# Convolution in 64x64 tiles: block states of odd channels computed across the array's halves

## The chip, the cores and the metric

The kernel runs on one core of one Trainium2 chip. The metric is the device time of one execution in microseconds (us). Three executions of the kernel before took 973.1, 973.68 and 978.77 us; their median is 973.68 us.

## The reference, cut to what matters

The input `x` is [8, 512, 256] (batch, steps, channels). A recurrence of 512 steps makes `u`. Then each channel of `u` goes through a causal convolution whose kernel is a sum of 64 decaying exponentials, and the result and a skip term are added to `x`:

```python
_, hs = jax.lax.scan(step, h0, jnp.swapaxes(xw, 0, 1))       # u: 512 steps, tanh
...
at = dt[:, None, None] * A[None, None, :] * t[None, :, None]
K = jnp.einsum('mn,mln->ml', C_re, jnp.exp(at))              # kernel of each channel
u_f = jnp.fft.rfft(u.transpose(0, 2, 1), n=2 * L_)
k_f = jnp.fft.rfft(K, n=2 * L_)
y = jnp.fft.irfft(u_f * k_f, n=2 * L_)[..., :L_]
return y.transpose(0, 2, 1) + u * D
...
x = x + _L0_attn_ref(_L0_cond_ref(x, ...), ...)
x = x + _L0_ffn_ref(_L0_cond2_ref(x, ...), ...)              # gated recurrence, then experts
```

The convolution is the part that the change touches.

## The kernel before, in words

The kernel is written with one instruction list per engine and semaphores between them, so the order in each list is the order in which that engine works. The stages are: the recurrence (products of 128x32 tiles, about 7 to 378 us), the convolution (about 379 to 448 us), the gated recurrence with routing and the shared network, and the 16 experts.

For the convolution the 512 steps of a batch are cut into 8 blocks of 64 steps (`HB`). The 256 channels are two halves of 128 (`k`), held in partitions 0 to 63 and 64 to 127 of one tile: partition rows are the 64 steps of a block, `rows_of_half(k)`. Channels are taken 8 at a time (`CP`), in 16 groups (`NCH`); the group's parity `z` picks the buffers. TensorE works with the array split into four tiles of 64x64; a tile is named by (its rows' start, its columns' start). The rows decide from which partitions it reads, the columns to which partitions of PSUM it writes. A float32 product of the program appears as two products in the trace. For each group of channels TensorE does three blocks of work:

- `own_block(z)` (L590): the block's own steps against a 64x64 Toeplitz matrix, 8 channels x 2 halves x even and odd blocks, 32 columns each. All four tiles are used in turn.
- `block_states(1 - z)` (L577): for the next group, the 64 state terms that each block leaves behind, 8 channels x 2 halves, 56 columns each. Half 0 uses tile (0, 0) and half 1 tile (64, 64); the other two tiles are not used. It writes bank 0 or bank 1 of PSUM, by the parity.
- `carried(z)` (L599): the states that come from earlier blocks, added onto the sums of `own_block`, 32 columns each, in all four tiles.

Between `block_states` and `carried` of a group VectorE carries the states over the blocks by a scan (`carry`, L1169), and after `carried` it adds the sums to `x` (`add_x`, L1175). One `block_states` stands ahead of the loop. GpSimd and ScalarE make the powers and decays of later groups (L393, L404, L892) and copy operands into the two slots that the loop can address (L897, L902); SyncE moves the Toeplitz matrices into their slots (L336). Each of the three blocks is led by `stand()` (L604): a product of zeros, 128 rows, 32 columns of the array, 8 columns streamed, that carries the semaphore wait.

Ahead of the loop 64 transposes of 128x128 (L565) turn the recurrence's output, and VectorE (L1160) and ScalarE (L905) copy it out of PSUM by turns. At the start of the kernel one DMA loads `pack`, a row of small operands, on ScalarE's queue.

Of the kernel before, what the change touches and what calls it, by code (L numbers as in the profile page):

```python
# [13 lines left out]
P = 128  # L14
B, S, D = 8, 512, 256
C = D // P
# [37 lines left out]
def build(nc, x_tok, x_steps, h0_gate, wx_d, wh_d, b_rec_d, pack_d,  # L54
# [5 lines left out]
    with ExitStack() as ctx:  # L60
# [3 lines left out]
        def sem(name):  # L64
            return ctx.enter_context(nc.semaphore(name))
# [5 lines left out]
        sizes = (C * B, NST, 1, P + KP, P, IT, KP * C * KP, 8, HB, RB, R + CT)  # L71
        pack = sb("pack", [P, sum(sizes)])
        h0r, a_bc, a_q, dt_q, c_q, d_k, masks, consts, iota_t, resets_t, rows_to = [pack[:, sum(sizes[:n]):sum(sizes[:n + 1])] for n in range(len(sizes))]
# [158 lines left out]
        s_own = sem("s_own")  # L232
        s_slot_tz = [sem("s_slot_tz0"), sem("s_slot_tz1")]
# [6 lines left out]
        block = ctx.enter_context(nc.Block())  # L240

# [142 lines left out]
        def _(pool):  # L384
# [7 lines left out]
            def power_args(m):  # L392
                pool.tensor_tensor(pw[:, m % 2], dt_q[:, CP * m:CP * m + CP].unsqueeze(2).to_broadcast([P, CP, NST]),  # L393
                                   a_bc.unsqueeze(1).to_broadcast([P, CP, NST]), ALU.mult).then_inc(s_pa, 1)
# [5 lines left out]
            pool.wait_ge(s_dtm, 3)  # L400
            for m in range(2):
                power_args(m)
            def block_decays(m):
                pool.tensor_tensor(d0[:, m % 2], lam[:, CP * m:CP * m + CP].unsqueeze(2).to_broadcast([P, CP, RB]),  # L404
                                   resets_t.unsqueeze(1).to_broadcast([P, CP, RB]), ALU.mult).then_inc(s_d0, 1)
# [72 lines left out]
        def _(pe):  # L478
# [115 lines left out]
            def carried(z):  # L594

                for c in range(CP):
                    for k in range(C):
                        for odd in range(2):
                            last = nc.tensor.matmul(to_tokens(z, c, k, odd), qd[rows_of_half(k), CP * z + c], xc[rows_of_half(k), z, c].rearrange("p (r e) -> p r e", e=2)[:, :, odd],  # L599
                                                    start=False, stop=True, skip_group_check=True, tile_position=(HB * k, HB * odd))  # L600
                last.then_inc(s_qmm, 1)
# [260 lines left out]
        def _(act):  # L862
# [6 lines left out]
            nc.scalar.activation(dt_q[:], dt_q[:], ACT.Exp).then_inc(s_dtm, 1)  # L869
            act.wait_ge(s_dta, 1)  # L870
# [245 lines left out]
        def _(dve):  # L1116
# [42 lines left out]
            nc.vector.memset(ps[:, 0:2].rearrange("p n (c t) -> p (n c) t", t=NB)[:, :, 0], 0.0).then_inc(s_xc, 1)  # L1159
# [332 lines left out]
```

## Time and profile before

| What | Value |
|---|---|
| median of three runs | 973.68 us (973.1 to 978.77) |
| the profiled execution's own time | 974.19 us |
| span in the profile, mean granted clock | 972.3 us, 0.978 |
| TensorE products busy | 924.3 us (95%) |
| VectorE, ScalarE, GpSimd busy | 410.7 (42%), 506.3 (52%), 299.1 us (31%) |
| recurrence, about | 7 to 378 us |
| transposes and copies | 379 to 388 us |
| convolution loop | 388 to 448 us |

The span is the time from the first to the last instruction; 1.9 us of the profiled execution lie around it. Busy times are sums over an engine's instructions; weight loads are counted apart as PEld and lie beside the products. "PEclk" in the profile is the clock that TensorE was granted, in parts of full speed: 1.00 is 2.4 GHz, 0.50 is 1.2 GHz.

### The profile page before, as it was taken

Reading aid. Unit: us, or ns where it says so; the run is one execution under the profiler, and the core shown is the slowest. Engines: PE = TensorE matmul, PEld = TensorE weight load, DVE = VectorE, ACT = ScalarE, POOL = GpSimd, SP = SyncE. Lnnn points to the kernel's source line nnn. Section 1 sums busy time; section 2 is a strip of 40 time slices with the busy share of each in tenths; the row PEclk is TensorE's granted clock in tenths of the full one; section 3 lists DMA queues with packets and bytes.
Section 4 is the critical chain, followed back from the end, with each engine's and each line's share of the span. In section 5 each row is a group of like instructions: output and inputs, shape, how many; then the busy total and the mean of one; then the engine's idle time right before and its main releaser. Section 6 shows DMA issues by size and latency. Waiting matters only on the chain.

```text
span 972.3 us, 64880 instructions
## 1 busy us (share of the span) xinstructions
PE 924.3 (95%) x28864; PEld 777.5 (80%) x28864; DVE 410.7 (42%) x781; ACT 506.3 (52%) x1735; POOL 299.1 (31%) x324
## 2 busy tenths in 40 slices
PE   7999999999999999999999998999899999999993
PEld 5888888888888888996444446788899999999993
DVE  1000010100001103553899799875564646556450
ACT  2444444444444446443876587134465656566551
POOL 3111111111111110650003463760045364554545
PEclk6799999999999999999999999999999999999997
DMA  2222222221111111111001110533357666675634
GB/s 89 83 92 87 95 93 87 100 85 33 35 40 36 35 33 28 66 76 57 0 1 39 49 56 22 184 116 108 127 132 162 133 157 119 151 146 127 134 40 53
DMA packets 69161, 80.34 MB, mean 83 GB/s; under 512 B 24225, under 2 KB 53558, under 8 KB 69122
## 3 DMA queue, kind: packets, MB, share of 16 engines
q1 hardware_dynamic: 54242, 62.18, 20.3%
q0 software_dynamic: 14592, 17.10, 10.7%
q8 instruction: 23, 0.38, 0.2%
q10 hardware_dynamic: 288, 0.56, 0.2%
q14 instruction: 16, 0.13, 0.0%
HBM read 44.16 MB, written 33.83 MB: 80 GB/s over the span
## 4 chain that ended last, share of the span: by engine, by line
PE 81%; issue 5%; ACT 4%; POOL 4%; DVE 3%; DMA 2%; POOLq 0%; SPq 0%; ACTq 0%; DVEq 0%
PE ps L516 19%; PE ps L811 16%; PE ps L508 9%; PE ps L825 8%; PE ps L677 8%; PE ps L489 6%; PE ps L727 3%; POOL slots_in L447 2%; PE ps L577 2%; ACT tok L879 2%; PE ps L590 2%; PE ps L736 2%; PE ps L599 2%; PE ps L494 2%; DMA slots_in<-tok,arena 1%
## 5 line engine op out<-in xcount | busy, mean ns | idle before, releaser
L516 PE MATMUL ps<-tok,wh 128*32 128x8 f32 x16384 | 255.2, 180 | 12.9 <-issue 3.5
L879 ACT ACTIVATE tok<-ps 128x8 f32<-128x8 f32 x1024 | 155.9, 177 | 204.0 <-PE ps L516 201.6
L516 PEld LDWEIGHTS ps<-tok,wh 128*32 128x32 f32 x16384 | 220.0, 113 | 48.0 <-ACT tok L879 25.2
L466 POOL DMA_INDIRECT out<-arena,dest x80 | 127.9, 1599 | 99.3 <-ACT arena L1030 76.9
L489 PE MATMUL ps<-zero 128*32 128x192 bf16 x1920 | 141.1, 255 | 0.0
L418 POOL TENSOR_TENSOR big<-tok,zero 128x128 f32 x64 | 29.0, 453 | 322.0 <-ACT tok L879 322.0
L811 PE MATMUL ps<-xgT_hi,ew_hi 128*128 128x320 f32 (+1 forms) x384 | 119.5, 311 | 3.2 <-DVE spare L1275 1.6
L811 PE MATMUL ps<-xgT_hi,ew_lo 128*128 128x320 f32 (+1 forms) x384 | 119.5, 311 | 0.0
L811 PE MATMUL ps<-xgT_lo,ew_hi 128*128 128x320 f32 (+1 forms) x384 | 119.0, 310 | 0.0
L1143 DVE TENSOR_TENSOR arena<-arena,pack 128x256 f32 x32 | 13.6, 426 | 246.3 <-ACT arena L884 246.3
L1381 DVE TENSOR_TENSOR mid<-mid,ps 128x320 f32<-128x320 f32 (+1 forms) x96 | 46.6, 486 | 107.0 <-ACT mid L1048 57.5
L677 PE MATMUL ps<-mid,gw 128*128 128x512 f32 x192 | 83.8, 593 | 2.5 <-ACT mid L958 1.6
L447 POOL DMA_INDIRECT slots_in<-tok,arena x64 | 73.1, 1142 | 23.6 <-issue 17.1
L1048 ACT ACTIVATE mid<-ps 128x320 f32<-128x320 f32 (+1 forms) x96 | 41.8, 435 | 73.9 <-PE ps L811 71.0
L508 PE MATMUL ps<-xst,wx 128*32 128x64 f32 (+1 forms) x3120 | 76.3, 209 | 0.0
L677 PEld LDWEIGHTS ps<-mid,gw 128*128 128x128 f32 x192 | 36.1, 190 | 46.5 <-issue 45.2
L811 PEld LDWEIGHTS ps<-xgT_hi,ew_hi 128*128 128x128 f32 (+1 forms) x384 | 69.2, 180 | 4.0 <-DVE spare L1275 1.9
L825 PE MATMUL ps<-ew_hi,eact_hi 128*128 128x256 f32 (+1 forms) x240 | 71.7, 299 | 0.3 <-ACT arena L1030 0.3
L489 PEld LDWEIGHTS ps<-zero 128*32 128x32 bf16 x1920 | 62.1, 96 | 11.5 <-issue 0.5
L811 PEld LDWEIGHTS ps<-xgT_lo,ew_hi 128*128 128x128 f32 (+1 forms) x384 | 69.4, 181 | 0.0
L811 PEld LDWEIGHTS ps<-xgT_hi,ew_lo 128*128 128x128 f32 (+1 forms) x384 | 69.3, 180 | 0.0
L825 PE MATMUL ps<-ew_lo,eact_hi 128*128 128x256 f32 (+1 forms) x240 | 67.8, 282 | 0.0
(206 smaller groups left out, 1643.5 us busy)
## 6 DMA issues: line engine op xcount, KB each, us to landing
slots_in<-mid SPq DMA_DIRECT2D x16, 645.0 KB, 3.7
mid<-slots_in SPq DMA_DIRECT2D x16, 645.0 KB, 4.2
arena<-in_ex_down SPq DMA_DIRECT2D x16, 384.0 KB
arena<-in_ex_gate SPq DMA_DIRECT2D x16, 352.0 KB
arena<-in_ex_up SPq DMA_DIRECT2D x16, 352.0 KB
xst<-in_x_steps SPq DMA_DIRECT2D x66, 64.0 KB, 1.8
xtok<-in_x_tok SPq DMA_DIRECT2D x16, 256.0 KB, 2.7
mid<-k_pad SPq DMA_DIRECT2D x32, 128.0 KB, 3.1
```

The source lines that it names most:

```text
L447: pool.indirect_dma_start(out=slots_in[:, :], out_offset=bass.IndirectOffsetOnAxis(ap=idx[:, k, r:r + 1], axis=0), in_=hid_tok[:, r, :], i ...
L466: pool.indirect_dma_start(out=out[:, :], out_offset=bass.IndirectOffsetOnAxis(ap=dest[:, z, t:t + 1], axis=0), in_=yo[:, z, t], in_offset= ...
L489: nc.tensor.matmul(ps[Q * j:Q * j + Q, 6, 0:columns], zero16[:, 0:Q], zero16[:, 0:columns], start=True, stop=True, tile_position=(0, Q * j))
L508: last = nc.tensor.matmul(ps[Q * j:Q * j + Q, to, 0:cols], w, v, start=c < 0, stop=c == C - 1, skip_group_check=True, tile_position=(0, Q ...
L516: last = nc.tensor.matmul(sums_at(bank, t, o)[Q * j:Q * j + Q], wh[:, k, columns(j, o)], hring[:, (n - 1) % (2 * G), k], start=False, stop ...
L677: last = nc.tensor.matmul(ps[:, gate_bank(n % NT, q), :], gw[:, q, c, z * P:(z + 1) * P], x1T[:, c, 4 * b:4 * b + 4, :].rearrange("p r t - ...
L727: last = nc.tensor.matmul(ps[0:fw, bank, :], of(w)[:, c, f0:f0 + fw], v, start=c == 0 and p == 0, stop=c == C - 1 and p == len(parts) - 1)
L811: last = nc.tensor.matmul(ps[0:fw, 2 * h + m % 2, 0:HALF], of(w)[:, c, f0:f0 + fw], v[:, c, hf * HALF:(hf + 1) * HALF], start=c == 0 and p ...
L825: last = nc.tensor.matmul(ps[:, 4 + (z + t) % 2, 0:D], a[0:fw, f, t * P:(t + 1) * P], down_of(w)[0:fw, f], start=f == 0 and p == 0, stop=f ...
L879: nc.scalar.activation(hring[:, n, o], sums_at(n // G, n % G, o), ACT.Tanh).then_inc(s_h[o], 1)
L1048: nc.scalar.activation(esil[0:fw, m % 2], ps[0:fw, m % 2, 0:HALF], ACT.Silu).then_inc(s_esil, 1)
L1381: nc.vector.tensor_tensor(eprod[0:fw, m % 2], esil[0:fw, m % 2], ps[0:fw, 2 + m % 2, 0:HALF], ALU.mult).then_inc(s_eact, 1)
```

## The change

The states of odd channels of a group are now computed in the two tiles that stood still: half 0 writes to partitions 64 to 127 and half 1 to partitions 0 to 63. So that two row halves never add into one bank at a time, the even channels' states lie in one bank and the odd ones' in the next (banks 0 and 1 for even groups, 6 and 7 for odd ones), and `carried` is split into the even and the crossed channels. Between the two parts the states of the next group are computed. Decays, kernels and masks of odd channels are laid out with their halves exchanged, for which `pack` gets 128 more columns (`dt_s`, the step sizes not exchanged) and ScalarE one more exponential. The wait product is now 128x128 with 128 columns and adds zeros to columns of a sum's bank that hold nothing. Ten products of zeros with 256 columns follow the transposes, and VectorE clears two more banks once the first transposes are done.

```diff
+        psf = ps[:, :, :].rearrange("p n t -> p (n t)")
+        def states_at(z):
+            return psf[:, 512 * 6 * z + 256:512 * 6 * z + 768]
+        def place_of(c):
+            return CP // 2 * (c % 2) + c // 2
...
-            pool.wait_ge(s_dtm, 3)
+            pool.wait_ge(s_dtm, 4)
...
+            pe.wait_ge(s_xc, 1)
+            for _ in range(5):
+                nc.tensor.matmul(ps[:, 0, 0:256], zero16[:, 0:P], zero16[:, 0:256], start=True, stop=True)
+                nc.tensor.matmul(ps[:, 0, 0:256], zero16[:, 0:P], zero16[:, 0:256], start=True, stop=True)
...
                 for c in range(CP):
                     for k in range(C):
-                        to = ps[rows_of_half(k), z, RB * c:RB * c + RB].rearrange("p (b t) -> p b t", t=NB)[:, :, 1:NB]
+                        h, at = k ^ c % 2, RB * place_of(c)
+                        to = states_at(z)[rows_of_half(h), at:at + RB].rearrange("p (b t) -> p b t", t=NB)[:, :, 1:NB]
                         last = nc.tensor.matmul(to, pw[rows_of_half(k), z, c], u_tok[rows_of_half(k), CP * z + c].rearrange("p (b t) -> p b t", t=NB)[:, :, 0:NB - 1],
-                                                start=True, stop=True, skip_group_check=True, tile_position=(HB * k, HB * k))
+                                                start=True, stop=True, skip_group_check=True, tile_position=(HB * k, HB * h))
...
-            def carried(z):
-                for c in range(CP):
-                    for k in range(C):
+            def carried(z, crossed):
+                for c in range(crossed, CP, 2):
+                    for h in range(C):
                         for odd in range(2):
...
+                last.then_inc((s_half, s_qmm)[crossed], 1)
...
-            def stand():
-                nc.tensor.matmul(ps[0:Q, 6, 0:B], zero16[:, 0:Q], zero16[:, 0:B], start=True, stop=True, tile_position=(0, 0))
+            def stand(z):
+                at = R * CP
+                nc.tensor.matmul(ps[:, 2 + 2 * z, at:at + P], zero16[:, 0:P], zero16[:, 0:P], start=False, stop=False, skip_group_check=True)
...
-                    stand()
+                    stand(z)
                     own_block(z)
+                    pe.wait_ge(s_xc, m + 2)
                     pe.wait_ge(s_pe, m + 2)
-                    pe.wait_ge(s_xc, m + 1)
                     pe.wait_ge(s_uea, 2 * m + SLOTS - 1)
-                    stand()
+                    stand(z)
+                    carried(z, 0)
                     block_states(1 - z)
-                    pe.wait_ge(s_xc, m + 2)
-                    pe.wait_ge(s_uea, 2 * m + SLOTS - 2)
-                    stand()
-                    carried(z)
+                    pe.wait_ge(s_half, m + 1)
+                    stand(z)
+                    carried(z, 1)
...
+            nc.scalar.activation(dt_s[:], dt_s[:], ACT.Exp).then_inc(s_dtm, 1)
...
-            nc.vector.memset(ps[:, 0:2].rearrange("p n (c t) -> p (n c) t", t=NB)[:, :, 0], 0.0).then_inc(s_xc, 1)
+            nc.vector.memset(ps[:, 0:2].rearrange("p n (c t) -> p (n c) t", t=NB)[:, :, 0], 0.0)
+            dve.wait_ge(s_utr, 1)
+            nc.vector.memset(ps[:, 6:8].rearrange("p n (c t) -> p (n c) t", t=NB)[:, :, 0], 0.0).then_inc(s_xc, 1)
...
-                nc.vector.tensor_tensor_scan(xc[:, z].rearrange("p c r -> p (c r)"), d0[:, z].rearrange("p c r -> p (c r)"), ps[:, z, :], 0.0, ALU.mult, ALU.add).then_inc(s_xc, 1)
+                nc.vector.tensor_tensor_scan(xc[:, z].rearrange("p c r -> p (c r)"), d0[:, z].rearrange("p c r -> p (c r)"), states_at(z), 0.0, ALU.mult, ALU.add).then_inc(s_xc, 1)
```

This is TensorE's list for one group of channels (`z` = 0) in the loop before. L604 is `stand`, L590 `own_block`, L577 `block_states`, L599 `carried`:

```order
L604 MATMUL ps<-zero 32x8 [waits s_slot_tz0]
L590 MATMUL ps<-tok,mid 64x32 x32
L619 REGISTER_ALU
L621 ISA [waits s_xc,s_pe]
L604 MATMUL ps<-zero 32x8 [waits s_uea]
L577 MATMUL ps<-tok,arena 64x8x7 x16
L625 REGISTER_ALU [waits s_xc]
L604 MATMUL ps<-zero 32x8 [waits s_uea]
L599 MATMUL ps<-arena 64x32 x32
```

And the same group in the changed kernel, where L621 is `stand`, L605 `own_block`, L614 `carried` and L592 `block_states`:

```order
L621 MATMUL ps<-zero 128x128 [waits s_slot_tz0]
L605 MATMUL ps<-tok,mid 64x32 x32
L636 REGISTER_ALU
L638 ISA [waits s_pe,s_xc]
L621 MATMUL ps<-zero 128x128 [waits s_uea]
L614 MATMUL ps<-arena 64x32 x16
L592 MATMUL ps<-tok,arena 64x8x7 x16
L621 MATMUL ps<-zero 128x128 [waits s_half]
L614 MATMUL ps<-arena 64x32 x16
```

The counts of products in the blocks are the same. Half of `carried` now stands ahead of the states without a wait product between them, and the wait for the scan of this group has moved from behind the states to ahead of them.

On VectorE, at the passage from the recurrence to the convolution, the list of the changed kernel reads as follows; the second row is new, and all eight copies stand behind it:

```order
L1177 MEMSET ps 128x128 [waits s_h1,s_h0]
L1179 MEMSET ps 128x128 [waits s_utr]
L1180 COPY tok<-ps 128x128x4 [waits s_utr] x8
L1189 SCALAR_TENSOR_TENSOR arena<-arena,ps 128x512 [waits s_d0,s_tmm,s_x]
L1189 SCALAR_TENSOR_TENSOR arena<-arena,ps 128x512 [waits s_d0,s_tmm]
L1195 TENSOR_TENSOR xtok<-ps,xtok 128x2x32x8 [waits s_qmm]
```

## Rows read from the trace of the kernel before

**Rows 1.** Windows by stage: stretch, length, busy us (records) of each engine, PEclk, DMA, GB/s.
```profile
7.70:35.00 27.30, 22.51 (x1049) 20.28 (x1050) 1.32 (x5) 8.08 (x51) 3.62 (x6) 0.50 0.17 55
35.00:62.00 27.00, 26.29 (x1729) 22.52 (x1731) 2.68 (x11) 12.37 (x81) 3.99 (x8) 1.00 0.30 105
...
379.00:388.00 9.00, 7.64 (x64) 7.43 (x64) 7.47 (x8) 7.74 (x10) 0.32 (x1) 1.00 0.01 2
388.00:448.00 60.00, 58.37 (x2640) 54.60 (x2640) 29.66 (x32) 27.66 (x45) 29.41 (x28) 1.00 0.17 62
```

**Rows 2.** Timeline of a period of the loop: start, length, engine, line, operation, count.
```profile
400.58 0.18 PE L604 MATMUL ps<-zero 128*32 128x8 bf16 x1
...
400.69 1.14 PE L590 MATMUL ps<-tok,mid 64*64 64x32 f32 x64
...
400.72 0.69 DVE L1175 TENSOR_TENSOR xtok<-ps,xtok 128x512 f32<-128x512 f32 x1
...
401.75 0.18 PE L604 MATMUL ps<-zero 128*32 128x8 bf16 x1
...
401.86 1.14 PE L577 MATMUL ps<-tok,arena 64*64 64x56 f32 x32
...
402.93 0.18 PE L604 MATMUL ps<-zero 128*32 128x8 bf16 x1
...
403.04 1.14 PE L599 MATMUL ps<-arena 64*64 64x32 f32 x64
403.05 1.22 DVE L1169 TENSOR_TENSOR_SCAN arena<-arena,ps 128x512 f32<-128x512 f32 x1 [1.64 <-PE ps L577]
```

**Rows 3.** Waits from 384 to 452 us: who waits for whom, us, times, longest.
```profile
PE ps L577 <- DVE tok L1160: 1.2, 1, 1.2
```

**Rows 4.** Groups of TensorE products, 374 to 452 us: busy, mean ns, idle before.
```profile
L577 PE MATMUL ps<-tok,arena 64*64 64x56 f32 x544 | 19.4, 221 | 1.2 <-DVE tok L1160 1.2
```

**Rows 5.** TensorE alone in equal stretches inside one `own_block`, then one `block_states`.
```profile
389.50:390.08 0.58, 0.58 (x49) 1.00 0.00 0
390.70:391.28 0.58, 0.58 (x25) 1.00 0.00 0
```

**Rows 6.** Timeline of products in tiles of 128x32: the router's, then the recurrence's.
```profile
501.30 1.07 PE L662 MATMUL ps<-big,rw 128*32 128x256 f32 x16 [0.26 <-ACT mid L920]
```
```profile
374.40 0.27 PE L489 MATMUL ps<-zero 128*32 128x192 bf16 x4
...
374.49 0.43 PE L516 MATMUL ps<-tok,wh 128*32 128x8 f32 x32
```

**Rows 7.** Weight loads of full width and of the wait product: ns min/median/max.
```profile
L484 PEld LDWEIGHTS ps<-zero x8: 105/147/147, 1.3 to 3.9; 128*128 128x128 bf16 x8
```
```profile
L604 PEld LDWEIGHTS ps<-zero x48: 92/92/93, 389.2 to 446.5; 128*32 128x32 bf16 x48
```

**Rows 8.** DMA issues, 388 to 452 us: KB each, median us to landing.
```profile
mid<-mid SPq DMA_DIRECT2D x14, 256.0 KB, 2.3
```

**Rows 9.** Timeline ahead of the loop.
```profile
378.79 0.17 DVE L1159 MEMSET ps<- 128x128 f32 x1 [5.13 <-ACT tok L879]
...
379.38 7.64 PE L565 MATMUL ps<-ident,big 128*128 128x128 f32 x64 [0.91 <-POOL big L418]
380.13 7.47 DVE L1160 COPY tok<-ps 128x512 f32<-128x512 f32 x8 [1.17 <-PE ps L565]
380.57 7.50 ACT L905 ACTIVATE tok<-ps 128x512 f32<-128x512 f32 x8 [1.26 <-PE ps L565]
...
388.18 1.14 PE L577 MATMUL ps<-tok,arena 64*64 64x56 f32 x32 [1.16 <-DVE tok L1160]
```

**Rows 10.** Start of the kernel: issues of the first 6 us, then the timeline.
```profile
pack<-in_pack ACTq DMA_DIRECT2D x1, 289.0 KB, 3.0
```
```profile
4.03 0.30 ACT L869 ACTIVATE pack<-pack 128x132 f32<-128x132 f32 x1
...
5.50 0.18 PEld L508 LDWEIGHTS ps<-spare,brow 1*32 1x32 f32 x8 [1.50 <-issue]
```

More of the change, by code:

```diff
@@ L70, in build @@
         h0g = sb("h0g", [P, C, B])
-        sizes = (C * B, NST, 1, P + KP, P, IT, KP * C * KP, 8, HB, RB, R + CT)
+        sizes = (C * B, NST, 1, P + KP, P, P, IT, KP * C * KP, 8, HB, RB, R + CT)
         pack = sb("pack", [P, sum(sizes)])
-        h0r, a_bc, a_q, dt_q, c_q, d_k, masks, consts, iota_t, resets_t, rows_to = [pack[:, sum(sizes[:n]):sum(sizes[:n + 1])] for n in range(len(sizes))]
+        h0r, a_bc, a_q, dt_q, dt_s, c_q, d_k, masks, consts, iota_t, resets_t, rows_to = [pack[:, sum(sizes[:n]):sum(sizes[:n + 1])] for n in range(len(sizes))]
         h0r = h0r.rearrange("p (c b) -> p c b", c=C)
@@ L232, in build @@
         s_own = sem("s_own")
+        s_half = sem("s_half")
         s_slot_tz = [sem("s_slot_tz0"), sem("s_slot_tz1")]
@@ L392, in power_args @@
             def power_args(m):
-                pool.tensor_tensor(pw[:, m % 2], dt_q[:, CP * m:CP * m + CP].unsqueeze(2).to_broadcast([P, CP, NST]),
+                pool.tensor_tensor(pw[:, m % 2], dt_s[:, CP * m:CP * m + CP].unsqueeze(2).to_broadcast([P, CP, NST]),
                                    a_bc.unsqueeze(1).to_broadcast([P, CP, NST]), ALU.mult).then_inc(s_pa, 1)
@@ L403, in block_decays @@
             def block_decays(m):
-                pool.tensor_tensor(d0[:, m % 2], lam[:, CP * m:CP * m + CP].unsqueeze(2).to_broadcast([P, CP, RB]),
-                                   resets_t.unsqueeze(1).to_broadcast([P, CP, RB]), ALU.mult).then_inc(s_d0, 1)
+                pool.tensor_tensor(d0[:, m % 2].rearrange("p (e c) r -> p e c r", e=2), lam[:, CP * m:CP * m + CP].rearrange("p (c e) -> p e c", e=2).unsqueeze(3).to_broadcast([P, 2, CP // 2, RB]),
+                                   resets_t.unsqueeze(1).unsqueeze(1).to_broadcast([P, 2, CP // 2, RB]), ALU.mult).then_inc(s_d0, 1)
             pool.wait_ge(s_lam, 1)
@@ L592, in own_block @@
                 last.then_inc(s_own, 1)
-            def carried(z):
-                for c in range(CP):
-                    for k in range(C):
+            def carried(z, crossed):
+                for c in range(crossed, CP, 2):
+                    for h in range(C):
                         for odd in range(2):
-                            last = nc.tensor.matmul(to_tokens(z, c, k, odd), qd[rows_of_half(k), CP * z + c], xc[rows_of_half(k), z, c].rearrange("p (r e) -> p r e", e=2)[:, :, odd],
-                                                    start=False, stop=True, skip_group_check=True, tile_position=(HB * k, HB * odd))
-                last.then_inc(s_qmm, 1)
-            def stand():
-                nc.tensor.matmul(ps[0:Q, 6, 0:B], zero16[:, 0:Q], zero16[:, 0:B], start=True, stop=True, tile_position=(0, 0))
+                            last = nc.tensor.matmul(to_tokens(z, c, h ^ crossed, odd), qd[rows_of_half(h), CP * z + c], xc[rows_of_half(h), z, place_of(c)].rearrange("p (r e) -> p r e", e=2)[:, :, odd],
+                                                    start=False, stop=True, skip_group_check=True, tile_position=(HB * h, HB * odd))
+                last.then_inc((s_half, s_qmm)[crossed], 1)
+            def stand(z):
+                at = R * CP
+                nc.tensor.matmul(ps[:, 2 + 2 * z, at:at + P], zero16[:, 0:P], zero16[:, 0:P], start=False, stop=False, skip_group_check=True)
             pe.wait_ge(s_uev, NB)
@@ L1446, with crossed @@
     masks = np.zeros((P, KP, C, KP), f32)
-    masks[:, np.arange(KP), :, np.arange(KP)] = (half[:, None] == np.arange(C))[None]
+    masks[:, np.arange(KP), :, np.arange(KP)] = (half ^ np.arange(KP)[:, None] % 2)[:, :, None] == np.arange(C)
     over = np.zeros((P, KP), f32)
+    def crossed(v):
+        w = v.reshape(C, P, -1).copy()
+        w[:, 1::2] = w[::-1, 1::2]
+        return w
     steps = x.reshape(B, S // G, G // 2, 2, C, P).transpose(1, 5, 4, 3, 2, 0).reshape(S // G, P, C, G, B)
@@ L1457 @@
     tri = np.stack([np.triu(np.ones((P, P)), 1) - 1, np.ones((P, P))], 1).astype(f32)
-    pack = (rows(cond.T), np.broadcast_to(a_log, (P, NST)), np.tile(a_log, C), np.concatenate([np.repeat(dt.reshape(C, P), HB, 0), over], 1),
-            c_re.reshape(C, P, NST).transpose(0, 2, 1), d_k, masks, consts, np.broadcast_to(-np.arange(HB, dtype=f32), (P, HB)),
+    pack = (rows(cond.T), np.broadcast_to(a_log, (P, NST)), np.tile(a_log, C), np.concatenate([np.repeat(crossed(dt)[:, :, 0], HB, 0), over], 1), np.repeat(dt.reshape(C, P), HB, 0),
+            crossed(c_re).transpose(0, 2, 1), d_k, masks, consts, np.broadcast_to(-np.arange(HB, dtype=f32), (P, HB)),
             np.broadcast_to((np.arange(RB) % NB > 0).astype(f32), (P, RB)),
```

## The prediction

> **What bounds the kernel now.** I read the windows by stage first. In the loop of the convolution, 388 to 448 us, TensorE is busy 58.37 of 60.00 us and every other engine under 30 [rows 1], and its granted clock is 1.00, the level of 2.4 GHz. So the stage lasts as long as TensorE's list. The view of waits agrees: the one wait of this stage's products is 1.2 us ahead of the first states [rows 3].
>
> The timeline of one period tells what the list costs [rows 2]. A wait product starts at 400.58, the own block at 400.69, the next wait product at 401.75, the states at 401.86, the next at 402.93, the carried block at 403.04. Each block with its wait product takes 1.17 to 1.18 us, of which 0.11 lie between the wait product's start and the block's. Three make a period of 3.53 us.
>
> The point is that 64 products of `own_block` and 32 of `block_states` both last 1.14 us. Less the 0.22 us of the last one (its mean is 221 ns [rows 4]), 0.92 us lie between the first start and the last: 0.92/63 = 14.6 ns for each product of the own block, 0.92/31 = 29.7 ns for each of the states. In equal stretches, 49 records stand against 25 [rows 5]. A turn over the tiles, four in one case and two in the other, takes 58 or 59 ns either way. The states' turn is as long although its products have 56 columns and not 32, so the columns are not what sets it, and two tiles stand still.
>
> **The change part by part.**
>
> *States in four tiles.* If a turn stays at 58 ns and holds four products, 32 products take 32 x 14.6 = 0.47 instead of 32 x 29.7 = 0.95 us: 0.48 less. 544 products [rows 4] are 17 blocks of 32, so 8.2 us less. The least saving is zero (the tiles run as pairs, below). More would need a turn under 58 ns, which neither block shows. Can four tiles stream 56 columns at once? The nearest rows say yes: 16 router products of 256 float32 columns in four tiles last 1.07 us together, the last one included [rows 6]. At 4 turns that is under 0.27 us a turn for 256 columns, so 56 columns in four tiles fit into 58 ns. And the own block reads both row halves for both column halves. I take 0.47 a block, 8.0 us, for the turn that starts a block is a little longer.
>
> *Wait products of 128 columns.* There are 48 before [rows 7] and 48 after, three to a group: the count of passages between the full array and the 64x64 tiles stays. Each streams 120 columns more. Four products of 192 columns hold the array for 0.09 us (374.40 to 374.49 [rows 6]), 0.47 ns a column with the passage, so 120 columns are 0.05 us, and 48 x 0.05 = 2.5 us more. Lower bound: nothing, if the columns run under the 0.11 us that each passage takes. Upper bound: 96 more weight columns at the same rate, 0.04 each, so 0.09 and 4.3 us. I take 2.5, since the weight load of full width takes 105 ns at least where that of 32 columns takes 92 [rows 7], 13 ns apart and not 40.
>
> The Trainium skill (TensorE: Matmul & The Clock Gate, LDWEIGHTS) puts a load at its columns divided by 1.2 ns: 107 for 128 and 27 for 32, 80 ns apart. By that the sum would lose 3.8 us more, and the gain would nearly go; the 13 ns between the two rows speak against it, in durations that hold the whole load.
>
> *The order of the list.* The products of a group are the same; half of `carried` and the states run on without a wait product between them. What moves is the wait for the scan. Before, the states' products of group m ended, and the scan (1.22 us, started about 0.26 after the last states' product: 401.86 + 0.92 = 402.78 against 403.05 [rows 2]) had a carried and an own block and more to run under. After the states of group m TensorE now has: passage 0.15, wait product 0.16, half a carried block 0.45, passage and wait product 0.31, own block 0.92, passage 0.15. That is 2.1 us (0.15 is 401.75 less 400.69 less 0.92; 0.16 is 0.11 plus 0.05). The scan is done after 0.26 + 1.22 + about 0.1 = 1.6 us. So 0.5 us remain, and the wait costs nothing in the steady loop. For the first group, where no carried block comes between, 0.15 + 0.16 + 0.92 + 0.15 = 1.4 us stand against 1.6: 0.2 us once. `add_x` (0.69 us) follows each scan, ends 2.3 us after the states and is not needed for 4 us; both together are 1.9 of a period of 3.2, so VectorE doesn't bound. The slot copies of the Toeplitz matrices land 2.3 us after their issue [rows 8] and have two periods less one block, 5.3 us. The wait for the even half is for products that ended 0.6 us earlier.
>
> *Zeros behind the transposes.* TensorE has 64 transposes at 379.38 for 7.64 us, so they end at 387.02, and the states start at 388.18 when ScalarE's copy, which ends at 388.07, is done [rows 9]. Ten products of 256 columns at 0.47 ns are 1.2 us. They can start a little before the last transpose ends, as the wait product at 401.75 does before the own block's end at 401.83 [rows 2], so at 386.9, and end at 388.1, with 0.1 for the passage to the tiles at 388.2: they fit, or are 0.1 late. Cover: ScalarE's last copy. I charge nothing, at most 0.2. The clearing of two more banks is 0.17 us ahead of VectorE's eight copies [rows 9]. VectorE's last copy then ends at 387.8, before ScalarE's 388.07; the transposes of later turns wait for it and can push ScalarE by at most 0.2. I take 0.1.
>
> *Start.* `pack` grows by 128 columns, 64 KB beside 289 [rows 10]. At that load's own rate (289 KB in 3.0 us) it is 0.66 us, an upper bound for the loads that TensorE's first product at 5.50 waits for; the exponential (0.30 us for 132 columns) stands on ScalarE 1.5 us before the first tanh can come. I take 0.2 us, bounds 0 and 0.7.
>
> **Sum**: -8.0 + 2.5 + 0.2 + 0.1 + 0.2 = -5.0 us. Against the profiled execution's 974.19 that is 969.2; the median of the runs shown is 0.5 lower, so **969.0 us**. Its own range, by the bounds of the wait products and the start: 966 to 972.
>
> **Rivals.**
>
> 1. *The tiles run as pairs* (slower). The four products of a turn write two banks, two row halves into each. If tiles of both row halves can't work into a bank at the same time, or the crossed tiles wait for the straight ones, a turn of four costs two turns of 58 ns and the states stay at 0.95. Then only the costs remain: +3.0 us, 976.7. The point from which the change loses is 3.0/17 = 0.18 us saved in a block. Against it: before, the two tiles of the states already write one bank from both row halves at the same turn as the own block. The Trainium skill (TensorEngine Tiling (Array Packing), Gotcha 1) says that "different row tiles cannot access same PSUM bank simultaneously"; by it the changed states would still go one half at a time, 976.7. The 25 records of [rows 5] don't look like it, but can't exclude it. Chance 13%.
> 2. *The wait products are dear*: at the upper bound of 0.09 us each, -8.0 + 4.3 + 0.5 = -3.2, so 970.5; with the dearer load of the page's rule about 972.8. Chance 12%.
> 3. *The clock*. At 0.50, the level of 1.2 GHz, 27.3 us held 1049 products where 27.0 us at 1.00 held 1729 [rows 1]: a stretch at half costs up to 0.4 to 0.5 of its length. Should the denser loop lose the clock for some microseconds, that is 1 to 3 us, so 970 to 972; should the slow stretch at the start, 27.3 us long and worth 10.7 us, end sooner or later in these runs, 966 or 972. Nothing in the stage hints at it: 1.00 before, in the transposes and in the loop. Chance 9%.
> 4. *A wait of the order*: if the scan or its release were 0.6 us later than I reckon, each period would be bound by it, and 16 periods lose 0.1 to 0.3 us each, 971 to 974. Chance 6%.
>
> **How the numbers follow.** The forecast has 60%. With its own 966 to 972, rivals 2 and 3 and most of 4, the range 965.5 to 975.5 leaves out rival 1 and the tails. Measured differences under 1% (9.7 us) can't be told from no change here; the run shown at 978.77 is 5 us off its neighbours. Faster by over 1% (under 964) needs the forecast and a shorter slow stretch at the start: 5%. Slower by over 1% (over 983.4) needs rival 1 and a lost clock: 3%. Within 1%: 92%.
>
> **What the profile of the changed kernel would show.** Right: the states' line with 32 products in about 0.7 us instead of 1.14, a period of 3.2 us instead of 3.53, wait products 0.16 ahead of their blocks, no TensorE wait for the scan but the first, the first states at 388.2 to 388.5, PEclk 1.00. Wrong: states still near 1.1 us (rival 1), wait products 0.2 ahead of their blocks (rival 2), "idle before" on the wait product with the scan as releaser (rival 4), or digits below 9 in PEclk between 379 and 445 us (rival 3).

## The result and the profile after

The changed kernel takes 1008.34 us (median of four executions, 1005.3 to 1010.01), the kernel before 973.9. The ratio is 1.033, 95% interval 1.029 to 1.037. The prediction of 969.0 with a range of 965.5 to 975.5 was wrong, and wrong in sign. One more thing is needed to read the numbers below: executions of one kernel can differ by 25 us and more, by whether TensorE's clock is lost in the loop.

The page of the changed kernel's profile shows where to look: a hole in TensorE's granted clock in the middle of the kernel, under a row of nines for its busy time (40 slices of 25.2 us, tenths).

```profile
PE   7999999999999999999999999999899999999994
...
PEclk6599999999999999555899999999999999999997
```

In windows that end where the clock changes (the others where the stage or the row of before does; stretch, length, busy us and records of PE, PEld, DVE, ACT, POOL, then PEclk, DMA share, GB/s):

```profile
7.70:35.00 27.30, 21.57 (x1007) 19.26 (x1006) 1.33 (x5) 7.75 (x48) 3.63 (x6) 0.50 0.17 55
35.00:52.00 17.00, 17.00 (x826) 15.38 (x818) 1.16 (x6) 5.92 (x39) 2.19 (x5) 0.50 0.21 72
```
```profile
393.37:400.20 6.83, 5.92 (x283) 5.16 (x285) 3.02 (x3) 3.25 (x6) 4.21 (x4) 1.00 0.12 41
400.20:480.50 80.30, 79.27 (x2371) 70.55 (x2363) 27.16 (x29) 24.63 (x39) 25.22 (x24) 0.50 0.12 43
480.50:488.95 8.45, 7.35 (x15) 3.86 (x16) 0.29 (x1) 1.20 (x2) 0.00 (x0) 0.50 0.39 132
```

The loop of the convolution starts at full clock, loses it at 400.2 us after seven microseconds and never gets it back: to the end of the loop and 8 us into the next stage TensorE stands at 0.50, the level of 1.2 GHz, busy for 79.27 of 80.30 us. The loop before had 1.00 throughout [rows 1]. In this execution the stretch at half clock at the start was also longer, 44.4 us where it was 27.3 [rows 1]; most of the 5.1 us by which the transposes start later (384.45 against 379.38 [rows 9]) goes with that. The loop's part is larger: from its first states to the next stage's first transposes it takes 87.5 us (393.37 to 480.85), and the time before was 60.4 (388.18 [rows 9] to 448.59). The next stage's first transposes, in the changed kernel, then before:

```profile
480.85 1.97 PE L653 MATMUL ps<-ident,xtok 128*128 128x128 f32 x8 [0.81 <-DVE xtok L1195]
```
```profile
448.59 1.09 PE L636 MATMUL ps<-ident,xtok 128*128 128x128 f32 x8 [0.81 <-DVE xtok L1175]
```

The timeline of TensorE in the loop's first pass (a pass is two groups of channels) and once the clock is lost (start, length, line, tiles, count, idle before):

```profile
393.37 0.69 PE L592 MATMUL ps<-tok,arena 64*64 64x56 f32 x32
...
397.53 0.23 PE L621 MATMUL ps<-zero 128*128 128x128 bf16 x1
...
397.69 0.66 PE L605 MATMUL ps<-tok,mid 64*64 64x32 f32 x28
...
399.01 0.77 PE L605 MATMUL ps<-tok,mid 64*64 64x32 f32 x36 [0.67 <-issue]
```
```profile
403.94 1.93 PE L605 MATMUL ps<-tok,mid 64*64 64x32 f32 x64
405.80 0.29 PE L621 MATMUL ps<-zero 128*128 128x128 bf16 x1
406.02 1.08 PE L614 MATMUL ps<-arena 64*64 64x32 f32 x32
406.90 1.10 PE L592 MATMUL ps<-tok,arena 64*64 64x56 f32 x32
407.93 0.29 PE L621 MATMUL ps<-zero 128*128 128x128 bf16 x1
408.15 1.08 PE L614 MATMUL ps<-arena 64*64 64x32 f32 x32
409.16 0.29 PE L621 MATMUL ps<-zero 128*128 128x128 bf16 x1
409.38 1.93 PE L605 MATMUL ps<-tok,mid 64*64 64x32 f32 x64
```

Two things are to be seen. At full clock 32 products of the states last 0.69 us and not 1.14 [rows 2], as forecast. And in the midst of an own block, where no semaphore is waited for, TensorE stands idle for 0.67 us with "issue" as the reason. The clock falls 1.2 us after it resumes. At half clock a period is 5.44 us (403.94 to 409.38) against 3.53 before.

The standstill has a companion in the view of DMA, the stretch 396.4 to 399.1 us by queue: packets, MB, share.

```profile
q1 hardware_dynamic: 144, 0.26, 26.6%
q8 instruction: 1, 0.02, 3.0%
```

One load of 16 KB of instructions starts at 396.47, and TensorE resumes 2.5 us later. The same pair stands in the loop's first pass before: a load at 391.38, and an idle time of 0.23 us in the same block, over at 393.90. I had seen that 0.23 and made nothing of it.

```profile
393.90 0.65 PE L590 MATMUL ps<-tok,mid 64*64 64x32 f32 x26 [0.23 <-issue]
```

### The profile page after: what moved, and what is told of

The parts are those of the page before. It is cut to its first block, busy times and chain, and to the rows that moved or that the text cites. A ratio compares the mean times of both kernels' runs of the same rounds, so it can differ in the third digit from the quotient of the medians.

```text
span 1008.2 us, 64886 instructions
## 1 busy us (share of the span) xinstructions
PE 960.2 (95%) x28874; PEld 805.7 (80%) x28874; DVE 410.9 (41%) x782; ACT 507.9 (50%) x1736; POOL 299.5 (30%) x324
## 4 chain that ended last, share of the span: by engine, by line
PE 87%; DVE 4%; ACT 4%; issue 3%; POOL 1%; DMA 1%; POOLq 0%; SPq 0%; ACTq 0%; DVEq 0%
PE ps L526 19%; PE ps L828 16%; PE ps L518 8%; PE ps L842 8%; PE ps L694 8%; PE ps L499 6%; PE ps L744 6%; PE ps L614 3%; PE ps L771 3%; PE ps L605 3%; PE ps L753 2%; ACT tok L897 2%; PE ps L504 2%; PE ps L592 1%; PE ps L621 1%
## 5 line engine op out<-in xcount | busy, mean ns | idle before, releaser
L526 PE MATMUL ps<-tok,wh 128*32 128x8 f32 x16384 | 258.6, 181 | 12.7 <-issue 4.0
L526 PEld LDWEIGHTS ps<-tok,wh 128*32 128x32 f32 x16384 | 224.0, 114 | 47.8 <-ACT tok L897 24.8
L694 PE MATMUL ps<-mid,gw 128*128 128x512 f32 x192 | 86.5, 609 | 2.4 <-ACT mid L976 1.6
```

Source lines behind the costliest of these rows:

```text
L526: last = nc.tensor.matmul(sums_at(bank, t, o)[Q * j:Q * j + Q], wh[:, k, columns(j, o)], hring[:, (n - 1) % (2 * G), k], start=False, stop ...
L694: last = nc.tensor.matmul(ps[:, gate_bank(n % NT, q), :], gw[:, q, c, z * P:(z + 1) * P], x1T[:, c, 4 * b:4 * b + 4, :].rearrange("p r t - ...
```

## The experiments

The question is what took the clock. The count of executions that lost it is given for each kernel; only one execution of each was traced, and the others are told by their time, where the two kinds are 25 us and more apart. The kernel before, which ran beside all of these, lost it too in 5 of 53 executions (1012.6 to 1015.1 us each, the rest 972.6 to 980.9), by the time alone: none of the five was traced.

**The wait products and the zeros.** Four kernels. `a_wait256` widens the changed kernel's wait products, `a_wait8` gives it those of before, `a_nozeros` drops the ten products behind the transposes, and `b_wait128` gives the kernel before the new wait products.

```diff
 # a_wait256, in the changed kernel
-                nc.tensor.matmul(ps[:, 2 + 2 * z, at:at + P], zero16[:, 0:P], zero16[:, 0:P], ...)
+                nc.tensor.matmul(ps[:, 2 + 2 * z, at:at + 2 * P], zero16[:, 0:P], zero16[:, 0:2 * P], ...)
 # a_wait8, in the changed kernel
+                nc.tensor.matmul(ps[0:Q, 2 + 2 * z, at:at + B], zero16[:, 0:Q], zero16[:, 0:B], ..., tile_position=(0, 0))
 # b_wait128, in the kernel before
-                nc.tensor.matmul(ps[0:Q, 6, 0:B], zero16[:, 0:Q], zero16[:, 0:B], ...)
+                nc.tensor.matmul(ps[:, 2 + 2 * z, at:at + P], zero16[:, 0:P], zero16[:, 0:P], ...)
```

> The changed kernel with wait products of 256 columns instead of 128, nothing else. Known so far: the changed kernel's loop ran as predicted for six microseconds (states in 0.67 us, wait products 0.16 ahead of their blocks) and then its granted clock fell to 0.50 at 400.2 us and stayed there for 88.8 us. Theory A (the loop keeps the array too little occupied to hold the clock once the states take half the time): more streamed columns in each period hold it at 1.00; the 128 more columns cost 48 x 0.055 = 2.6 us and the time is about 1010 - 31 + 2.6 = 981, or 972 if the slow stretch at the start is also as short as before. Theory B (the pauses of the loop's first pass, 0.67 and 0.41 us without an instruction between 398 and 403 us, start the fall whatever the loop does): the clock falls again near 400 us and the time stays over 1000.

> The changed kernel with the wait products of before (128 rows, 32 columns of the array, 8 streamed). Theory A: the array is occupied still less, so the clock falls at least as early, and at half clock a period is shorter by 3 x about 0.1 us of wait products: 1003 to 1010. Theory C (the passage to a product over the full array is what lowers the clock): it holds at 1.00 and the time is near 967.

> The changed kernel without the ten products of zeros behind the transposes. If they do nothing for the clock of the loop, it falls near 400 us all the same and the time is that of the change, 1005 to 1010. If they delay the fall, it comes one stretch earlier, near 394 to 397 us, and costs 1 to 2 us more.

> The kernel before with only the wait products changed to the full array and 128 columns. Prediction's term: 48 x 0.05 = 2.5 us more, 976.4. Theory C: the clock falls in the loop and the time is over 1000. Theories A and B: it holds, since the states still take 1.14 us in pairs.

Measured: `a_wait256` 1007.6 to 1008.8 us, the clock lost in all three executions that count (a fourth took 2634.6 us and tells nothing); `a_wait8` 1004.7 and 1001.9, lost in both; `a_nozeros` 1005.6 and 1008.8, lost in both. `b_wait128` has a median of 979.05 and lost it once in ten; its ratio, lost executions left out, is 1.0034 (1.0015 to 1.0052), so +3.3 us. Theory C is out: the wait products cost about what they were charged and take no clock. Theory A's remedy, more columns, did nothing; but the standstill of `a_wait256` was longer too, 1.32 us, so this run doesn't decide between A and B. The traces of the three losers all have the standstill, before the clock falls and not after. In `a_wait8`, then in `a_wait256`:

```profile
396.20 0.66 PE L605 MATMUL ps<-tok,mid 64*64 64x32 f32 x28
398.36 0.77 PE L605 MATMUL ps<-tok,mid 64*64 64x32 f32 x36 [1.50 <-issue]
```
```profile
395.90 0.59 PE L614 MATMUL ps<-arena 64*64 64x32 f32 x25
397.81 0.31 PE L614 MATMUL ps<-arena 64*64 64x32 f32 x7 [1.32 <-issue]
```

**Pairs, padding, and a standstill made in the kernel before.**

`a_pairs` mixes up the sums of the odd channels: it leaves out their exchange of halves, and its work is otherwise that of the changed kernel.

```diff
 # a_pairs, in the changed kernel
-                        h, at = k ^ c % 2, RB * place_of(c)
+                        h, at = k, RB * place_of(c)
 # a_pad4 (range(4)) and a_pad10 (range(10)), in the changed kernel
+                    if z == 1:
+                        for _ in range(4):
+                            nc.tensor.matmul(ps[:, 4, R * CP:512], zero16[:, 0:P], zero16[:, 0:256], start=False, stop=False, ...)
                     own_block(z)
 # b_pause, on VectorE in the kernel before (b_pause2: range(12))
             for m in range(NCH + 1):
+                if m == 1:
+                    for _ in range(8):
+                        link(nc.vector.memset(spare[:, 128:512], 0.0))
```

> The changed kernel with the states of odd channels left in the straight tiles, so that two tiles work at a time again while the order, the banks and the wait products are the changed ones (channels' sums are then mixed up: the convolution's result is left wrong, its work is the same). Theory A' (it is the short states block that costs the clock, through the pauses of the first pass or through the occupation of the array): the states take 1.14 us again, the pause in the first pass shrinks to about 0.45 us as in the kernel before, the clock holds in most runs and the time is 974 + 3 = 977. Rival (order, banks or wait products cost the clock): it falls near 400 us and the time is over 1005.

> The changed kernel with four more products of zeros (full array, 256 columns, 0.11 us each) ahead of every second own block, there where the engine ran out of instructions in the first pass (0.67 to 1.7 us without an instruction in the four variants that lost the clock, 2.5 to 3 us after an instruction DMA began). Theory B (the pause of the first pass starts the fall): the pause shrinks by 0.44 us to about 0.45, the length it has in the kernel before, the clock mostly holds, and the time is 969 + 8 x 0.44 = 972.6. Rival A (the loop is too thinly occupied once the states are short): the added columns are fewer than those of the 256-column wait products, which did not help, so the clock falls and the time is about 1010.

> The same with ten such products, 1.1 us ahead of every second own block. Theory B: no pause over 0.3 us is left in the first pass, the clock holds at 1.00 to the end of the loop, and the time is 969 + 8 x 1.1 = 978. Rival A: half of the time of a pair of groups is as thin as before; if the clock falls it is over 1015.

> The kernel before, in which VectorE clears an unused tile eight times (about 4 us) ahead of the second scan, so that TensorE stands still for about 1.2 us once, in the loop's first pass, ahead of its second carried block; nothing of the loop's work changes. Theory B: the clock falls to 0.50 within a few us and stays there to the end of the loop: about 974 + 1.2 + 35 to 40 = 1012. Rival (only the changed loop loses the clock): it holds and the time is 975.5.

Measured: `a_pairs` 1015.0 and 1017.3, lost in both. `a_pad4` 1010.5, lost in all four. `a_pad10` 981.25 (977.7 to 986.7), none of the eight near 1010; the traced one, 977.7, kept the clock. Three took 984.6 to 986.7, where 978 was expected, and a short loss in them isn't excluded (`n_pad4w8` below has one). `b_pause` 977.1, lost in 2 of 8.

So theory A' fell: with the states back in pairs the clock goes all the same. The trace of `a_pairs` shows a standstill as long as that of the changed kernel, and a second one 3 us on:

```profile
396.59 1.13 PE L592 MATMUL ps<-tok,arena 64*64 64x56 f32 x32
...
397.82 0.59 PE L614 MATMUL ps<-arena 64*64 64x32 f32 x25
399.09 0.31 PE L614 MATMUL ps<-arena 64*64 64x32 f32 x7 [0.68 <-issue]
```

`a_pad4` missed for a reason that the trace shows too: its added products did not shorten the standstill behind them (0.68 us still), and a second one of 1.25 us came at the end of the pass, over at 402.18; the clock fell at 403.36. With ten, the one left was 0.52 us. And `b_pause` made only 0.62 us of standstill, not 1.2, which didn't decide anything.

**The order, a start ahead of the loop, and a long standstill.**

```diff
 # a_order, in the changed kernel
-                    pe.wait_ge(s_xc, m + 2)
                     pe.wait_ge(s_pe, m + 2)
                     pe.wait_ge(s_uea, 2 * m + SLOTS - 1)
                     stand(z)
-                    carried(z, 0)
                     block_states(1 - z)
+                    pe.wait_ge(s_xc, m + 2)
+                    stand(z)
+                    carried(z, 0)
 # a_pre, in the changed kernel
             block_states(0)
+            for _ in range(8):
+                nc.tensor.matmul(ps[:, 2, 0:512], zero16[:, 0:P], zero16[:, 0:512], start=True, stop=True)
```

> The changed kernel with its blocks in the order of before: own block, states of the next group, wait for the scan, even carried, crossed carried. The crossed tiles, the banks, the zeros and the wait products stay; a fourth wait product and passage come to each group (+0.3 us), so at full clock a period is 3.5 us and the time about 974. The change's order makes TensorE wait for the first scan before the first carried block, and its list of instructions is then taken up later. Theory D (that order lengthens the pauses for instructions in the first pass): pauses come down to under 0.5 us and the clock holds, 972 to 977. Rival (crossing, banks or the amount of code do it in any order): two pauses of 0.7 us and more, the clock falls, over 1005.

> The changed kernel with eight products of zeros of 512 columns (1.7 us in all) between the first states and the loop: the scan is done before the first carried block, and the sequencer can take up instructions while they run. Theory D: the pauses shrink, the clock holds, and the time is 969 + 1.7 = 971, faster than both kernels. Rival (the pauses come from a code that is used up faster than it is loaded, wherever it starts): the pauses stay at 0.7 us and more, the clock falls, about 1009.

> The kernel before with VectorE's unused clearing twelve times (6.1 us) ahead of the second scan, so that TensorE stands still once for some 2.5 us in the loop's first pass. With eight clearings the standstill was 0.62 us and the clock fell in 2 of 8 executions, against 4 of 37 of the unchanged kernel. Theory B (a long enough standstill starts the fall, and the loop can't win the clock back): it falls in most executions, and the time is about 974 + 2.5 + 36 = 1012. Rival: it holds, 977.

`b_pause2` is the test that shows that a standstill can be the trigger: 1012.9 us in both executions, with the loop's code, order and tiles those of the kernel before. TensorE in its first pass:

```profile
395.13 1.14 PE L577 MATMUL ps<-tok,arena 64*64 64x56 f32 x32
398.71 0.18 PE L604 MATMUL ps<-zero 128*32 128x8 bf16 x1 [2.43 <-DVE arena L1169]
398.82 1.93 PE L599 MATMUL ps<-arena 64*64 64x32 f32 x64
...
400.80 1.93 PE L590 MATMUL ps<-tok,mid 64*64 64x32 f32 x64
```

One standstill of 2.43 us, the clock falls 0.1 us before it ends (398.61), and each block takes 1.93 us from then on. The clock is back at 490.77, in the next stage, 92 us later. So the old loop didn't win its clock back either; it only seldom loses it. `a_order` lost it in three of four (977.3 in the one that kept it), with a standstill of 0.97 us: the order of before did not shorten the standstill, so theory D fell. `a_pre` kept it in two of four, 973.0 and 972.35, and lost it in the others, 1006.1 and 1005.1. The traced one is of those that kept it, although its first pass holds standstills of 0.53 and 0.76 us, longer than the one of the change:

```profile
400.04 0.43 PE L614 MATMUL ps<-arena 64*64 64x32 f32 x15 [0.76 <-issue]
```

**Fewer instructions, shorter standstills.** Without the ten zeros TensorE's list is 20 instructions shorter, and in `a_nozeros` the second standstill was gone.

```diff
 # n_pre1: a_nozeros, and
             block_states(0)
+            for _ in range(1):
+                nc.tensor.matmul(ps[:, 2, 0:512], zero16[:, 0:P], zero16[:, 0:512], start=True, stop=True)
 # n_pre1_pad (range(2)) and n_pad4w8 (range(4), and the wait products of a_wait8), besides
+                    if z == 1:
+                        for _ in range(2):
+                            nc.tensor.matmul(ps[:, 4, 0:512], zero16[:, 0:P], zero16[:, 0:512], start=True, stop=True)
                     own_block(z)
```

> The changed kernel without the ten zeros behind the transposes (20 instructions less in TensorE's list, after which only one pause stood in the first pass, of 1.18 us) and with one product of zeros of 512 columns (0.21 us) ahead of the loop, which covers most of the first scan. Theory B: one pause of 0.8 to 1.0 us is left, less than the 1.18 that lost the clock in both executions and without a second one near it, so the clock mostly holds: 969 + 0.2 = 969 to 971, in some executions 1006. Rival (a pause of this length is enough, or the changed loop doesn't hold the clock): over 1004 in all.

> The same with two more products of zeros of 512 columns (0.43 us) ahead of every second own block, the place just ahead of the pause. Theory B: the pause is 0.4 to 0.6 us, the clock holds in all executions, and the time is 969.2 + 8 x 0.43 = 972.6, about that of the kernel before. Rival (what holds the clock is the number of columns in every pass, ten products of 256 being enough and four not): the 1024 columns here are as many as those four products had, so it falls, over 1008.

> The same with four such products (0.85 us) and the short wait products of before, so that the odd groups have less work in the array per microsecond than in any variant, while the pause of the first pass is nearly gone. If only the pause matters the clock holds: 969.2 - 2.5 + 8 x 0.85 = 973.5. If the changed loop at its own pace is too thin to hold the clock, it falls somewhere in the loop, not necessarily in its first pass, and the time is over 1000.

`n_pre1` is a little faster than the kernel before: median 971.25 us, five executions at 969.9 to 972.7 and one lost at 1007.3; the ratio, lost executions left out, is 0.9953 (0.9924 to 0.9983). It differs from `a_nozeros`, which lost the clock in both executions with a standstill of 0.96 us, by a single product of zeros ahead of the loop. Its own standstill is 0.22 us, as short as before's:

```profile
396.79 0.77 PE L602 MATMUL ps<-tok,mid 64*64 64x32 f32 x37
397.78 0.65 PE L602 MATMUL ps<-tok,mid 64*64 64x32 f32 x27 [0.22 <-issue]
```

`n_pre1_pad` fell against the expectation, in all four (1010.9 to 1014.1). Two more products ahead of the place were to shorten the standstill, and lengthened it:

```profile
393.09 0.77 PE L602 MATMUL ps<-tok,mid 64*64 64x32 f32 x35
394.63 0.66 PE L602 MATMUL ps<-tok,mid 64*64 64x32 f32 x29 [0.78 <-issue]
```

It has more columns in each pass than `n_pre1` and loses the clock; that speaks once more for the standstill and against the work in the loop. The clock fell at 397.06, 2.4 us after this standstill. But four instructions in one place change the length of a standstill in a way that I can't predict. `n_pad4w8` missed as well: two executions at 988, two at 1015. Its profile (988.2) gives windows of a kind seen nowhere else:

```profile
389.74:392.00 2.26, 2.01 (x98) 1.86 (x99) 1.22 (x1) 0.51 (x2) 1.21 (x2) 1.00 0.00 0
392.00:422.70 30.70, 29.70 (x820) 25.18 (x826) 9.08 (x10) 9.74 (x16) 11.39 (x11) 0.50 0.12 45
422.70:447.00 24.30, 23.56 (x1116) 20.43 (x1114) 11.87 (x13) 12.22 (x20) 13.55 (x13) 1.00 0.20 76
```

It lost the clock at 392.00, 1.3 us after its first wait product (390.68), ahead of any standstill inside a block. Ahead of its first states it had waited 1.27 us for the last copy of the transposes, and it stood still for 0.25 us behind them. `n_pre1` had the same 1.27 us there, and the kernel before 1.16 [rows 9], and both kept the clock. It won it back in the loop, at 422.72, in the own block behind a burst of 2048 columns of zeros, which stands in every second group. From there on it kept it to the loop's end, with the short wait products of `a_wait8`.

The kernels together, each with the longest idle time of the loop's first pass in the one execution that was traced (`n_pad4w8` is left out, since its clock fell at the start of the pass):

| Kernel | longest idle, us | lost the clock |
|---|---|---|
| b_wait128 | none shown | 1 of 10 |
| before | 0.23 | 5 of 53 |
| n_pre1 | 0.22 | 1 of 6 |
| a_pad10 | 0.52 | 0 of 8 |
| b_pause | 0.62 | 2 of 8 |
| the change | 0.67 | 4 of 4 |
| a_pairs | 0.68 | 2 of 2 |
| a_pre | 0.76 | 2 of 4 |
| n_pre1_pad | 0.78 | 4 of 4 |
| a_nozeros | 0.96 | 2 of 2 |
| a_order | 0.97 | 3 of 4 |
| a_pad4 | 1.25 | 4 of 4 |
| a_wait256 | 1.32 | 3 of 3 |
| a_wait8 | 1.50 | 2 of 2 |
| b_pause2 | 2.43 | 2 of 2 |

The two columns rise together, but not strictly: 0.67 us in the change goes with a lost clock in four of four, 0.76 in `a_pre` with two of four. The idle time is that of one execution only, and in `b_wait128` the trace shows none in the pass.

## Why the prediction was wrong

**The states in four tiles: right.** `n_pre1`, which keeps the clock, shows the term at its own size. Groups of TensorE products (busy, mean ns, idle before):

```profile
L589 PE MATMUL ps<-tok,arena 64*64 64x56 f32 x544 | 11.4, 221 | 1.3 <-DVE tok L1179 1.3
```

11.4 us against 19.4 [rows 4] are the 8.0 us forecast. The rule of the Trainium skill that I set as a rival (TensorEngine Tiling (Array Packing), Gotcha 1: different row tiles can't use one bank of PSUM at the same time) did not show itself: two row halves write each bank here, on different partitions, and four products still share a turn. The trace disagrees with it as I had read it. The text on the change says that two row halves never add into one bank at a time; that holds for `carried`, and not for the states, where both halves write each bank in the same turn. That they don't go one after the other can be estimated from the next stage of `n_pre1`:

```profile
449.30 3.70 PE L693 MATMUL ps<-mid,gw 128*128 128x512 f32 x8 [0.82 <-ACT mid L937]
```

Eight products of 512 columns with starts about 0.44 us apart make 48 ns for 56 columns, and two of those in a row are more than a turn of 58.

**The wait products: right.** They start 0.16 us ahead of their blocks instead of 0.11, in the steady loop of `n_pre1`:

```profile
400.67 1.13 PE L602 MATMUL ps<-tok,mid 64*64 64x32 f32 x64
401.74 0.23 PE L618 MATMUL ps<-zero 128*128 128x128 bf16 x1
401.90 0.67 PE L611 MATMUL ps<-arena 64*64 64x32 f32 x32
402.39 0.67 PE L589 MATMUL ps<-tok,arena 64*64 64x56 f32 x32
402.99 0.23 PE L618 MATMUL ps<-zero 128*128 128x128 bf16 x1
403.15 0.67 PE L611 MATMUL ps<-arena 64*64 64x32 f32 x32
403.75 0.23 PE L618 MATMUL ps<-zero 128*128 128x128 bf16 x1
```

A period is 3.23 us (400.67 to 403.91) where I had 3.20. The charge was 2.5 us, `b_wait128` measured 3.3. The Trainium skill's rule for weight loads (TensorE: Matmul & The Clock Gate, LDWEIGHTS) would have made it 0.13 and not 0.05 us each; the trace says 0.05. The prediction had set the least of eight loads of full width, 105 ns, against 92, though their median was 147 [rows 7]; in the loop of `n_pre1` the loads of the wait products have a mean of 95 ns, so the reading came out right, but its row was a weak ground for it.

**Order, zeros and start: right but for the pass that comes first.** The first scan kept TensorE 0.24 us (0.2 forecast), no other scan did. In the changed kernel the zeros ended with ScalarE's last copy (393.28 and 393.26 us), so they fitted with nothing to spare. The term for the start can't be read from the times, since the stretch at half clock there is 27.3 us in some executions and 44.4 in others. By the traces TensorE's recurrence starts at 5.77 us and not 5.53, 0.24 later (0.2 forecast); over all traces it is 5.43 to 5.85 with the new start and 5.33 to 5.60 with the old. The price that the prediction gave the slow stretch, 10.7 us for 27.3, is too high. In the 17 us from 35 to 52 the changed kernel, at 0.50, has 826 records, and the kernel before, at 1.00, 1090: a quarter less. The same stretch before, then in `n_pre1`:

```profile
35.00:52.00 17.00, 16.53 (x1090) 14.06 (x1088) 1.61 (x7) 7.63 (x51) 2.51 (x5) 1.00 0.29 105
```
```profile
35.00:52.00 17.00, 17.00 (x818) 15.19 (x815) 1.36 (x7) 5.92 (x39) 2.59 (x5) 1.00 0.25 88
```

The second is shown at 1.00, yet has the records of the half clock: in the first 50 us of some traces PEclk misses the slow stretch, and the durations have to be looked at too. In the loop the two agree in every trace. Two slips of the sum are small: 0.5 under 969.2 is 968.7 and not 969.0, and 48 x 0.05 is 2.4.

The whole loop of `n_pre1`, first states to next stage, takes 54.9 us (392.47 to 447.39) against 60.4, so -5.5: my -8.0 + 2.5. It ends here:

```profile
447.39 1.09 PE L652 MATMUL ps<-ident,xtok 128*128 128x128 f32 x8 [0.81 <-DVE xtok L1194]
```

Over the executions that kept the clock its median is 971.21 us and that of the kernel before beside it 974.69, so 3.5 us less, where I had 5.0.

**The step that failed is rival 3**: "Nothing in the stage hints at it", a chance of 9% and a price of 1 to 3 us. Both halves were wrong. The price: a lost clock stays lost to the end of the loop, so it is the loop's length that counts, not "some microseconds". The ratio itself was good: a period takes 5.44 us at 0.50 and 3.23 at 1.00, so 0.41 of the 88.8 us at half are lost, 36 us, and that is the miss but for some 3 us. The prediction's 3% for a time over 983.4 also asked for rival 1 together with a lost clock; the lost clock alone was enough. Its own sign for this rival, digits below 9 in PEclk between 379 and 445 us, is what the page of the profile shows. `n_pre1` and the change differ by 32.6 us in the loop and by 37 in the median. I had the ratio of the rates at the two levels [rows 1] and multiplied it by too short a time. The chance: the loop before is itself near the edge (5 of 53), and the run at 978.77 was the only sign of spread that I had. What brings it over, as far as the runs show, is not the thinner work, which I would have guessed after the fact: `n_pre1` has that work and kept the clock in five of six executions, and `a_pairs` has the thick states of before and lost it. The runs point to standstills of the first pass that the changed list of instructions has and the old one has shorter. The rows of before had one of them, 0.23 us of "issue" inside an own block with an instruction load ahead of it.

What is shown, and what is only argued: that a standstill takes the clock from the unchanged loop, and that this loop then stays at half, is shown by `b_pause2`, in both of its executions. That the changed loop can keep the clock at its own pace is shown by `n_pre1`; `a_pad10` adds 2560 columns of zeros to every second group and can't show it. That the losses of the change come from the standstills is argued, from the table and from two pairs, `n_pre1` against `a_nozeros` and against `n_pre1_pad`; no run shortened the standstill of the changed kernel and left all else as it was. Length alone doesn't decide: 0.62 us in the old loop (`b_pause`) took the clock in 2 of 8 and 0.67 in the change in 4 of 4, while the traced `a_pre` kept it over 0.76. That the standstills are waits for instructions is inferred: they are in the midst of a block, only in the first pass, and end 2.3 to 3.1 us after an instruction load starts. Open is what sets their length (four added instructions made 0.22 into 0.78), and why `n_pad4w8` lost the clock without one, and why `a_pre` and `a_order` lose the clock in some executions and not in others.

## What to carry to other kernels

In a loop of small products the price of a short standstill can grow with the length of the loop (36 us here), if it takes TensorE's clock and the loop doesn't win it back: so read the granted clock next to every idle time before a dense stage is made shorter, and price its loss over the whole stage. The first pass of a loop can have costs of its own, idle times marked "issue" near an instruction load; a change that speeds the loop up, or only adds instructions ahead of it, can lengthen them. Where the time has two values 30 us apart, count executions before a median is believed.

## What the runs showed of the hardware

- Four tiles of 64x64 take a product each in the 58 ns in which two tiles did, with 56 float32 columns, two row halves and two banks: 32 products in 0.67 to 0.69 us against 1.14.
- TensorE can be busy by its records for 79.27 of 80.30 us in small products and stay at 0.50; the same blocks, in `n_pre1`, stayed at 1.00 from 392.47 to 447.39 us. The clock came back in the next stage, in products of 512 columns, at 488.95 us, and in one kernel within the loop, at 422.72 us, behind a burst of 2048 columns of zeros.
- A wait product over the full array costs 0.16 us ahead of 64x64 tiles, one over 32 columns of the array 0.11.
